# Layer 1 delta-rule attention: convolution stage and token-layout stage written as one program

## The reference, cut to what matters

```
def _causal_depthwise_conv_silu(x, w):      # K = 4 taps
    xp = jnp.pad(x, ((0, 0), (K - 1, 0), (0, 0)))
    y = sum((xp[:, i:i + l, :] * w[:, i] for i in range(K)))
    return _silu(y)

q = _causal_depthwise_conv_silu(hidden_states @ q_w, conv_q_w)
k = _causal_depthwise_conv_silu(hidden_states @ k_w, conv_k_w)
v = _causal_depthwise_conv_silu(hidden_states @ v_w, conv_v_w)
...
beta = jax.nn.sigmoid(hidden_states @ b_w)
...
g = jax.nn.sigmoid(hidden_states @ mix_w + mix_b + mix_bias)[..., None]
```

## Time and profile before

| | |
|---|---|
| median of 3 runs | 2727.68 us (2725.4 to 2728.22) |
| the profiled execution, its own time | 2730.1 us |
| its span, first to last instruction | 2728.3 us |
| mean granted TensorE clock over the span | 0.784 of full |
| busy share of the span | PE 70%, DVE 65%, ACT 42%, POOL 26% |

### The profile page before, as it was taken

The page is one execution under the profiler, slowest core; times in us unless marked ns, Lnnn a source line. Parts: engine busy times, 40 slices in busy tenths (PEclk is TensorE's granted clock), DMA queues, the critical chain, the costliest instruction groups (busy, mean ns, idle before and its releaser), DMA issues. The chain is left out here.

```text
span 2728.3 us, 36010 instructions
## 1 busy us (share of the span) xinstructions
PE 1919.4 (70%) x11227; PEld 1118.5 (41%) x11238; DVE 1772.2 (65%) x5568; ACT 1145.4 (42%) x3146; POOL 698.8 (26%) x601
## 2 busy tenths in 40 slices
PE   5987869853868999979885835555555555555777
PEld 2644427442345666634352513333233333324353
DVE  4235313258755666557555577999999999955535
ACT  3553332241315666621414623555555555541311
POOL 1200050405432333300021401333333333321220
PEclk8998789866989999979887966666666666666778
DMA  4000010400000000000200000000000000000000
GB/s 180 1 1 0 25 34 22 127 25 1 2 2 1 1 1 0 0 0 0 89 2 0 1 0 0 1 1 1 1 1 1 1 1 1 1 0 0 1 1 16
DMA packets 10064, 37.03 MB, mean 14 GB/s; under 512 B 1755, under 2 KB 7008, under 8 KB 8752
## 3 DMA queue, kind: packets, MB, share of 16 engines
q1 hardware_dynamic: 7856, 31.69, 3.0%
q0 software_dynamic: 2048, 3.38, 0.6%
HBM read 30.11 MB, written 5.77 MB: 13 GB/s over the span
## 5 line engine op out<-in xcount | busy, mean ns | idle before, releaser
L3445 PE MATMUL psum<-work 32*128 32x256 f32 x512 | 131.4, 658 | 296.8 <-ACT work L3540 296.8
L3592 DVE MATCH_REPLACE8 work<-work 128x256 f32<-128x256 f32 x768 | 305.5, 409 | 0.0
L3640 POOL TENSOR_TENSOR work<-work 128x1024 f32<-128x1024 f32 x64 | 150.7, 2355 | 515.0 <-ACT work L3540 515.0
L3589 DVE MAX8 work<-work 128x8 f32<-128x256 f32 x768 | 266.8, 410 | 0.0
L3445 PEld LDWEIGHTS psum<-work 32*128 32x128 f32 x512 | 78.1, 313 | 324.1 <-ACT work L3540 166.9
L626 POOL TENSOR_TENSOR work<-work 128x256 f32<-128x256 f32 (+2 forms) x144 | 133.5, 946 | 259.5 <-DVE work L886 259.5
L816 ACT ACTIVATE work<-work 128x128 f32<-128x128 f32 (+1 forms) x320 | 144.9, 454 | 38.5 <-PE psum L686 25.3
L309 DVE RECIPROCAL work<-work 128x256 f32<-128x256 f32 x38 | 66.5, 1749 | 121.2 <-ACT work L365 121.2
L3540 ACT ACTIVATE work<-work 128x256 f32<-128x256 f32 x256 | 128.2, 501 | 0.0
L3468 PE MATMUL psum<-work,tiles 128*8 128x256 f32 x512 | 117.0, 609 | 13.6 <-ACT work L3549 13.6
L3642 POOL TENSOR_TENSOR work<-work 128x1024 f32<-128x1024 f32 x64 | 121.2, 1894 | 6.2 <-DVE work L3614 1.2
(11 more groups left out here) (595 smaller groups left out, 4703.3 us busy)
## 6 DMA issues: line engine op xcount, KB each, us to landing
big_weights<-L0f_dram SPq DMA_DIRECT2D x1, 6053.5 KB, 25.4
big_weights<-L_dram SPq DMA_DIRECT2D x1, 5892.0 KB, 18.0
big_weights<-L_dram SPq DMA_DIRECT2D x1, 4952.5 KB, 15.6
big_weights<-L_dram SPq DMA_DIRECT2D x1, 2091.0 KB, 20.1
big_weights<-L_dram SPq DMA_DIRECT2D x1, 1630.5 KB, 11.5
big_weights<-L0f_dram SPq DMA_DIRECT2D x1, 1630.5 KB, 6.5
slots_in<-tiles SPq DMA_DIRECT2D x1, 1280.0 KB, 9.3
residual<-x_dram SPq DMA_DIRECT2D x1, 1024.0 KB, 4.7
```

The source lines that it names most:

```text
L3445: mm = nc.tensor.matmul(scores(n)[:, u, :], qb[head, tile % 2, u % 2 * P:(u % 2 + 1) * P], kb[head, tile % 2, :], start=True, stop=True, t ...
L3589: ch.step(v.max(top8[:, n % 2, u, r, :], src[:, u, :]))
L3592: ins = v.match_replace(raw[:, n % 2, u, :], top8[:, n % 2, u, r, :], src[:, u, :], REPLACED)
L3640: ch.link(g.tensor_tensor(mine, mine, rest[:, n % 2], ALU.subtract))
```

## The change

`conv_stage` and `delta_tokens` are replaced by one function, `conv_tokens`, with one block and thus one barrier less. The same arithmetic is done on the same engines, in another order:

- The convolutions go queries, keys, values. Each Silu is followed at once by its Square, for queries and keys.
- PE adds the heads of the queries after the first Square, turns the keys as soon as their Silu is done, adds the heads of the keys, and turns the values at the end. The head sums of the queries go to PSUM bank 6, those of the keys to a free part of bank 7, beside the gate logits.
- DVE shifts the gates between the first and the second convolution. ACT's Sigmoid follows the first Square.
- The root is taken by two Sqrt instructions of 128x128 instead of one of 128x256, after the four key groups are copied and before the Silu of the values.
- Two 128x1 Silu instructions ("warm") are added, which make the Silu table load happen before the wait for the next convolution. ACT has five table loads here instead of three.
- Of the eight groups ACT copies six (0 to 4 and 6) and DVE two (5 and 7).

The diff, without the two functions that it takes out (they stand above) and without lines of the new one that are the same as there:

```diff
@@ conv_stage and delta_tokens are taken out whole @@
-def conv_stage(c, tensors, taps):
...
-def delta_tokens(c, k, v, squares, kt, vt, gates, lengths, inv, sizes):
...
+def conv_tokens(c, q, k, v, taps, kt, vt, gates, lengths, inv, sizes):
+
+
+    nc = c.nc
+    H = 8
+    a = Arena(c)
+    tensors = (q, k, v)
+    acc = [a.take(N) for _ in tensors]
+    squares = a.take(2, N)
+    warm = a.take(1)
+    ps_g = c.psum[:, 7, 0:2 * P].rearrange("p (n e) -> p n e", e=2 * H)
+    ps_q = c.psum[:, 6, 0:P].rearrange("p (g h) -> p g h", h=H)
+    ps_k = c.psum[:, 7, 2 * P:3 * P].rearrange("p (g h) -> p g h", h=H)
+    groups = [(src, dst, t, b0) for src, dst in ((k, kt), (v, vt)) for t in range(2) for b0 in (0, 4)]
+    by_vector = (5, 7)
...
+    half = [slice(t * B * H, (t + 1) * B * H) for t in range(2)]
+
+    def bank(n):
+        return c.psum[:, n % 6, :].rearrange("p (k x) -> p k x", x=P)
+
...
+    with nc.Block() as block:
+        @block.tensor
+        def _(pe):
+            def add_heads(n, sums):
+                pe.wait_ge(c.squared.sem, c.squared.at(n + 1))
+                for g in range(NT):
+                    t, b = g // B, g % B
+                    mm = nc.tensor.matmul(sums[:, g, :], squares[:, n, b * S + t * P:b * S + (t + 1) * P], c.w("L1a_heads"),
+                                          start=True, stop=True)
+                mm.then_inc(c.lengths_ready.sem, 1)
+
+            def turn(n):
+                src, _, t, b0 = groups[n]
+                if n >= 6:
+                    pe.wait_ge(c.tokens_kept_s.sem, c.tokens_kept_s.at(n - 5))
+                for i in range(4):
+                    lo = (b0 + i) * S + t * P
+                    mm = nc.tensor.transpose(bank(n)[:, i, :], src[:, lo:lo + P], c.w("identity"))
+                mm.then_inc(c.tokens_turned.sem, 1)
+
+            for n in range(NT):
+                b, t = n // 2, n % 2
+                for r in range(4):
+                    lo = b * S + t * P + 32 * (r ^ (b % 4))
+                    mm = nc.tensor.matmul(ps_g[32 * r:32 * r + 32, n, :], c.HN[:, lo:lo + 32], c.w("L1a_gates"),
+                                          start=True, stop=True, tile_position=(0, 32 * r))
+            mm.then_inc(c.gate_logits.sem, 1)
+            add_heads(0, ps_q)
+            pe.wait_ge(c.permuted.sem, c.permuted.at(2))
+            for n in range(4):
+                turn(n)
+            pe.wait_ge(c.gates_shifted.sem, c.gates_shifted.at(1))
+            add_heads(1, ps_k)
+            pe.wait_ge(c.permuted.sem, c.permuted.at(3))
+            for n in range(4, 8):
+                turn(n)
+
+        @block.vector
+        def _(dve):
+            chain = Chain(dve, c.vector_chain)
+            vec = nc.vector
+
+            def convolve(n):
+                x, w, y = tensors[n], taps[n], acc[n]
+                K = w.shape[1]
+                xs = x.rearrange("p (b s) -> p b s", s=S)
+                ys = y.rearrange("p (b s) -> p b s", s=S)
+                chain.link(vec.tensor_scalar(y, x, w[:, K - 1:K], None, ALU.mult))
+                for back in range(1, K):
+                    ins = vec.scalar_tensor_tensor(ys[:, :, back:], xs[:, :, 0:S - back], w[:, K - 1 - back:K - back],
+                                                   ys[:, :, back:], ALU.mult, ALU.add)
+                    if back < K - 1:
+                        chain.link(ins)
+                ins.then_inc(c.convolved.sem, 1)
+
+            convolve(0)
+            dve.wait_ge(c.gate_logits.sem, c.gate_logits.at(1))
+            chain.link(vec.tensor_tensor(gates, ps_g, mix_b, ALU.add))
+            vec.tensor_tensor(gates, gates, mix_bias, ALU.add).then_inc(c.gates_shifted.sem, 1)
+            convolve(1)
+            convolve(2)
+            dve.wait_ge(c.rooted.sem, c.rooted.at(1))
+            chain.link(vec.reciprocal(inv, lengths))
+            dve.wait_ge(c.gates_ready.sem, c.gates_ready.at(1))
...
+            for n in by_vector:
+                _, dst, t, b0 = groups[n]
+                dve.wait_ge(c.tokens_turned.sem, c.tokens_turned.at(n + 1))
+                vec.tensor_copy(dst[:, t, b0:b0 + 4, :], bank(n)).then_inc(c.tokens_kept_v.sem, 1)
+            chain.clear()
+
+        @block.scalar
+        def _(act):
+            def soften(n):
+                x, y = tensors[n], acc[n]
+                act.wait_ge(c.convolved.sem, c.convolved.at(n + 1))
+                for j in range(4):
+                    for lo, at, count in moves(j):
+                        w = slice(0, 32 * count)
+                        src = blocks(y)[:, :, j, :, lo:lo + count, :].rearrange("p g t r s -> p g t (r s)")
+                        dst = blocks(x)[:, :, j, :, at:at + count, :].rearrange("p g t r s -> p g t (r s)")
+                        ins = nc.scalar.activation(dst[:, :, :, w], src[:, :, :, w], ACT.Silu)
+                ins.then_inc(c.permuted.sem, 1)
+
+            def square(n):
+                act.wait_ge(c.permuted.sem, c.permuted.at(n + 1))
+                nc.scalar.activation(squares[:, n, :], tensors[n], ACT.Square).then_inc(c.squared.sem, 1)
+
+            def keep(n):
+                _, dst, t, b0 = groups[n]
+                act.wait_ge(c.tokens_turned.sem, c.tokens_turned.at(n + 1))
+                nc.scalar.copy(dst[:, t, b0:b0 + 4, :], bank(n)).then_inc(c.tokens_kept_s.sem, 1)
+
+            soften(0)
+            square(0)
+            act.wait_ge(c.gates_shifted.sem, c.gates_shifted.at(1))
+            nc.scalar.activation(gates, gates, ACT.Sigmoid).then_inc(c.gates_ready.sem, 1)
+            nc.scalar.activation(warm, c.w("one"), ACT.Silu)
+            soften(1)
+            square(1)
+            for n in range(4):
+                keep(n)
+            act.wait_ge(c.lengths_ready.sem, c.lengths_ready.at(2))
+            nc.scalar.activation(lengths[:, P:2 * P], c.psum[:, 6, 0:P], ACT.Sqrt, bias=c.w("eps12"))
+            nc.scalar.activation(lengths[:, 0:P], c.psum[:, 7, 2 * P:3 * P], ACT.Sqrt, bias=c.w("eps12")) \
+                .then_inc(c.rooted.sem, 1)
+            nc.scalar.activation(warm, c.w("one"), ACT.Silu)
+            soften(2)
+            for n in (4, 6):
+                keep(n)
...
@@ in layer1_attention @@
-    squares = conv_stage(c, [k, v, q], [c.w(f"L1a_conv_{s}") for s in "kvq"])
-    delta_tokens(c, k, v, squares, kt, vt, gates, lengths, inv, sizes)
+    conv_tokens(c, q, k, v, [c.w(f"L1a_conv_{s}") for s in "qkv"], kt, vt, gates, lengths, inv, sizes)```

PE's order. Before, from the gate logits (L2082) on; L2143 are the head sums, L2152 the transposes, L2249 the first transposes of `delta_solve`:

```order
L2082 MATMUL psum<-big_weights,normed_input 32x16 x64
L2075 UNCONDITIONAL_BRANCH
L2138 UNCONDITIONAL_BRANCH [waits barrier_Pool_Activation_PE_DVE_SP_release]
L2143 MATMUL psum<-big_weights,work 128x8 x32
L2152 MATMUL psum<-small_weights,tiles 128x128 x24
L2152 MATMUL psum<-small_weights,tiles 128x128 [waits tokens_kept_s]
L2152 MATMUL psum<-small_weights,tiles 128x128 x3
L2152 MATMUL psum<-small_weights,tiles 128x128 [waits tokens_kept_v]
L2152 MATMUL psum<-small_weights,tiles 128x128 x3
L2137 UNCONDITIONAL_BRANCH
L2243 UNCONDITIONAL_BRANCH [waits barrier_Pool_Activation_PE_DVE_SP_release]
L2249 MATMUL psum<-small_weights,work 128x128 x16
```

More of the change, by code:

```diff
@@ L2803, in delta_finish, with blocks, moves @@
         s.advance(n)
+def conv_tokens(c, q, k, v, taps, kt, vt, gates, lengths, inv, sizes):
[11 more added lines that the diff above has]
+    by_vector = (5, 7)
+    mix_b = c.w("L1a_mix_b").unsqueeze(1).broadcast_to([P, NT, 2 * H])
+    mix_bias = c.w("L1a_mix_bias").unsqueeze(1).broadcast_to([P, NT, 2 * H])
+    half = [slice(t * B * H, (t + 1) * B * H) for t in range(2)]
+    def bank(n):
+        return c.psum[:, n % 6, :].rearrange("p (k x) -> p k x", x=P)
+    def blocks(x):
+        return x.rearrange("p (g j t r s) -> p g j t r s", j=4, t=2, r=4, s=32)
+    def moves(j):
+        if j == 0:
+            return [(0, 0, 4)]
+        if j == 2:
+            return [(0, 2, 2), (2, 0, 2)]
+        return [(r, r ^ j, 1) for r in range(4)]
+    with nc.Block() as block:
[57 more added lines that the diff above has]
+            dve.wait_ge(c.gates_ready.sem, c.gates_ready.at(1))
+            inv_k = inv[:, 0:P]
+            beta = gates[:, :, 0:H].rearrange("p (b t) h -> p t b h", t=2)
+            for t in range(2):
+                chain.link(vec.tensor_tensor(sizes[:, 1, half[t]].rearrange("p (b h) -> p b h", h=H),
+                                             inv_k[:, half[t]].rearrange("p (b h) -> p b h", h=H), beta[:, t], ALU.mult))
+            chain.link(vec.scalar_tensor_tensor(sizes[:, 0, :], inv_k, -1.0, sizes[:, 1, :], ALU.mult, ALU.mult))
+            for n in by_vector:
[39 more added lines that the diff above has]
+                keep(n)
+    for s, n in ((c.gate_logits, 1), (c.convolved, 3), (c.permuted, 3), (c.squared, 2), (c.lengths_ready, 2),
```

(5 more changed lines are left out.)

62 lines of the change are left out of this document (removed).

## The result

The changed kernel takes 2710.9 us (median of 6 runs, 2705.64 to 2714.58), the kernel before, in the same measurement, 2726.92 us (6 runs, 2724.68 to 2731.19). The ratio is 0.994, with a 95% interval of 0.9927 to 0.9953: 16 us faster, between 13 and 20.

The account below looks back on a forecast made before the run. In this stretch DVE then ACT set the pace with PE idle, then PE alone. Overlap saves 11.9 us, the solve's start loses 0.9: net 11.0, from the 2727.7 median to 2716.7 us; range 2711 to 2720.

Parts of the forecast that it names:

- The overlap: Convolution stage: PE's head sums and transposes run beside DVE and ACT work; stage ends at 596.7 instead of 608.6, 11.9 us saved.
- the new bottleneck: ACT waits about 5 us for key head sums with the values' Silu queued behind; 7.3 us of possible saving lost.
- The clock at the key head sums: PE's key head sums, behind the keys' transposes, were to run at clock 0.50 and take 6.83 us.
- I follow the chain that ends last, at the low clock (0.50): Whole new stage: PE's head sums and transposes timed at 0.2133 us each, the low-clock pace.
- the rivals at 2713.6 us: Early clock rise: keys' transposes raise the clock, key head sums take 3.76 us, 3.1 us more saved; chance 0.32.
- The solve's start: Solve's first 16 transposes: some run at the low clock, costing 0.9 us, bounds 0 and 1.5.
- Nine slow ones: Nine of the solve's 16 transposes at 0.095 us more each, as if the clock rose after 5.3 us of transposes.
- Everything behind it the same: Stages after the solve's start: expected unchanged, so the barrier passes the stage's saving on whole.
- The chances: Forecast 0.50, early clock 0.32, drain 0.04, warming sums 0.03, smaller gain 0.05, no change 0.03, slower 0.03; range leaves out 0.15.
- Table loads: ACT's table switches: 1.28 us each without drain; rival adds a 1.38 us drain per switch, 2719.5 us, chance 0.04.
- Engines hindering each other: Rival: PE's weight loads beside DVE's multiply-adds slow both; gain gone at 1.5 times, 2738.7 us at twice; chance 0.03.
- Head sums as warmers: Rival: head sums raise PE's clock by themselves, 3.1 and another 1.5 us saved, about 2712 us; chance 0.03.

Follow-up runs that it names:

- silu_first: Changed kernel with ACT's Silu of the values ahead of the two Sqrt, saving one 128x1 Silu and one table load; ratio 0.9916, stretch 38.87 us.
- one_block: Kernel before with its two old functions joined in one block, all instructions in the old order; ratio 1.0002, stretch 55.66 us.
- Silu_warm: silu_first with ACT also copying group 5, plus filler transposes (80, 15, 12); median 2710.26 us, ratio 0.9942, stretch 37.24 us.
- warm: Changed kernel plus unread filler transposes: 80 before and 15 behind query head sums, 36 behind key head sums; 2708.61 us, ratio 0.9937, stretch 39.62 us.
- the first group: First four follow-up kernels measured together (a_again, one_block, silu_first, split_turns); the kernel before took 2741.33 us there, and the stage began at 571.6 to 574.9 us.
- before_again: Kernel before, unchanged, run for a second profile; 2723.65 us, ratio 0.9991, stretch 55.73 us.
- split_turns: Changed kernel with half the key head sums placed between the first and last eight of the keys' transposes; ratio 0.9967, stretch 45.01 us.
- after: Profile of the changed kernel from the first measurement, against the kernel before; median 2710.9 us, ratio 0.994, stretch 41.45 us.
- a_again: Changed kernel measured again with no edit; ratio to the kernel before 0.9959, stretch 41.68 us.

## Why the prediction was wrong

- **The overlap: right.** The chain is the one forecast: second convolution, keys' Silu, keys' transposes, key head sums, Sqrt, table load, values' Silu, values' transposes, last copy. The keys' Silu was to start 17.63 us into the stage and started at 17.53; the wait of ACT before the values' Silu, forecast as the new bottleneck that leaves 7.3 us on the table, is there, but smaller: ACT waited 1.90 us instead of about 5, and 3.9 us stayed on the table, because the sums that it waits for ran 3.0 us faster. silu_first took all of the 3.9. one_block shows that the block's joining is worth nothing.
- **The clock at the key head sums: wrong, and the largest part of the miss.** The step that failed is "I follow the chain that ends last, at the low clock (0.50)", with the rise placed after 5.3 us of unbroken transposes. The rise came 3.0 to 3.8 us after the first transpose, in each of eight profiles. The sums took 3.95 us in the profile after, 3.7 to 4.0 in the eight, not 6.83. The case stood among the rivals at 2713.6 us with a chance of 0.32; its stretch, 14.1 us shorter, is the measured one to 0.1 us. Part of that agreement is luck: up to the solve's start the stage gained 15.45 us instead of the 15.0 of this case, and the solve's start lost 1.33 instead of 0.9. In hindsight I gave the wrong row more weight: the nearer one was that of sixteen records in an earlier stage (3.6 us), not that of the old order of this stage. Why the rise took 5.3 to 6.0 us there and less here stays open. By itself this step would have left the time inside the range; the remaining 2.7 us, from 2713.6 to 2710.9, are below.
- **The solve's start: right mechanism, mis-sized.** "Nine slow ones" of sixteen, 0.9 us; in fact all or all but the last ran slow (598.55 - 595.22 = 3.33 us to PE's next transposes instead of 1.88), and the stretch's end shows 1.33 us (4.15 from PE's first transpose to DVE's first work, before 2.82). Silu_warm and warm got it back.
- **"Everything behind it the same": wrong.** The later stages are the same instructions but not the same time. Behind the stretch the profiles of unchanged code differ by up to 11 us (2106.7 to 2118.0), and the stage itself begins up to 3.5 us earlier or later within the kernels measured outside the first group. The range that I gave this was nothing. It is large enough to make the 16.0, 9.5 and 18.1 us that three comparisons of medians show for the same stretch. How the 1.9 us beyond the stretch in the first comparison came about is not settled: the 6.7 us by which the profile after is shorter behind the stretch cannot be put down to the change, since before_again is 6.6 us shorter there too, and the interval, 13 to 20 us, holds 14.1. The other 0.8 of the 2.7 us is that the kernel before measured 2726.92 here and 2727.68 when I forecast. That the time fell 0.1 us outside the range and not inside is chance; the faster sums are not.
- **The chances: a slip.** The range holds the cases at 0.50, 0.32, 0.04 (2719.5) and 0.03 (about 2712), 0.89 together, and not 0.85.
- **Table loads: right.** By the Trainium skill (ScalarE: Activation LUTs, What ACT_TABLE_LOAD costs) a drain comes on top of each switch. Here the load at 586.23 ends at 587.51 and the next ACTIVATE starts at 587.52; no run shows the drain.
- **Engines hindering each other: did not happen.** The head sums beside DVE's multiply-adds kept the pace of the head sums alone: 6.99 us for 32 records against 13.79 for 64.
- **Head sums as warmers: did not happen.** The Trainium skill (TensorE: Matmul & The Clock Gate, The HAM clock gate) says that sustained matmul activity releases the throttle. The trace of split_turns does not show it for this mix: PE was busy for 11.7 of 12 us at 0.50, with 8-column matmuls for more than half of it.

## What to carry to other kernels

When a change moves a stage in time, judge it by the stage's own length in the trace, and check the stages around it before adding up: a gain of a microsecond or two can be given back or doubled elsewhere, in part by clock steps further down, so medians rank such versions by accident. Look at single executions too, since those of one kernel can fall into two groups. The order of PE's small work can decide at which clock it runs: a run of sixteen transposes sped up the sums behind it, two runs of eight did not, and a run of sixteen behind idle time did not speed up the work behind it either. So try the order and read the granted clock. On an in-order engine look at what is queued behind a wait, not only at how long it is: the Sqrt's wait cost only because the values' Silu stood behind it.

## What the runs showed of the hardware that was not expected

- 128x8 matmuls with a new 128x128 weight each, 0.213 us a record at the low clock, were not followed by a rise of TensorE's clock in 13.6 us without a gap. Sixteen 128x128 transposes at the same pace, behind 7 us of such matmuls, were, 3.0 to 3.8 us after the first of them in eight profiles of eight; eight in a row in the same place were not, and the values' sixteen, behind idle time, were followed by one only after 7.9 us or more.
- The clock fell again at about 584.8 in the profile after, with PE busy without a gap since 578.35 and for 0.7 us more. A busy PE did not keep it up there.
- Four later stages of the same code can repeat within 0.04 us between executions in different measurements, and can differ by 5.3 us between two executions of one kernel (scan, after and a_again). Across all versions the scan took 85.6 to 93.6 us. Two delay kernels show how little the medians follow the edit: with 1.9 us of memsets 2719.18 us, with 2.8 us 2713.29, while three of the former's ten executions took 2708.4 to 2714.2.
